# A decoder layer on one core: attention outputs divided two units at once, a later normalisation, outputs ahead of ranks at the end, and rows placed in three portions

## The reference

```python
# x, ctx: (128, 64, 128) f32; LN is layernorm without scale and shift
x = LN(x + self_attention(x))        # 8 heads, blocks of 64 rows, biases
x = LN(x + cross_attention(x, ctx))  # 16 heads of 8 columns, a mask of bytes
probs = softmax(x @ Wr.T)            # 8 experts
vals, idx = top_k(probs, 2); w = vals / vals.sum(-1)
h = silu(einsum('btd,efd->btef', x, W1)); y = einsum('btef,edf->bted', h, W2)
x = LN(x + sum over the two experts of w * y)
```

## Time and profile before

| | us |
|---|---|
| median of 3 runs (lowest to highest) | 1175.23 (1173.22 to 1178.68) |
| the profiled execution | 1175.13 |
| its span, first to last instruction | 1173.3 |

### The profile page before, as it was taken

The page is one execution under the profiler, slowest core; times in us unless marked ns, Lnnn a source line. Parts: engine busy times, 40 slices in busy tenths (PEclk is TensorE's granted clock), DMA queues, the critical chain, the costliest instruction groups (busy, mean ns, idle before and its releaser), DMA issues. The chain is left out here.

```text
span 1173.3 us, 31174 instructions
## 1 busy us (share of the span) xinstructions
PE 940.2 (80%) x11091; PEld 835.9 (71%) x11092; DVE 854.6 (73%) x2668; ACT 712.7 (61%) x1193; POOL 432.5 (37%) x527
## 2 busy tenths in 40 slices
PE   3888888888789989898989897685009999999991
PEld 2677776777678778787878686574009999999991
DVE  3687878788878888888888886666605767776772
ACT  3666667576477766666766556342007777877781
POOL 3142423324410111111111123543262777777674
PEclk9898889898899998999999979796559999999996
DMA  5940000000001000000000000000012322332220
GB/s 162 210 69 19 18 9 18 9 18 18 13 13 24 13 13 13 13 11 11 11 11 11 12 5 22 31 22 17 10 55 62 69 67 67 70 70 61 51 44 0
DMA packets 103727, 42.26 MB, mean 36 GB/s; under 512 B 58291, under 2 KB 99517, under 8 KB 103669
## 3 DMA queue, kind: packets, MB, share of 16 engines
q1 hardware_dynamic: 98676, 32.94, 13.8%
q0 software_dynamic: 4992, 8.54, 2.3%
HBM read 20.68 MB, written 16.57 MB: 32 GB/s over the span
## 5 line engine op out<-in xcount | busy, mean ns | idle before, releaser
L897 ACT ACTIVATE pr<-psum 128x512 f32<-128x512 f32 x192 | 114.1, 594 | 107.7 <-PE psum L604 102.7
L1107 DVE TENSOR_TENSOR at<-psum,rc 64x32 f32<-64x32 f32 (+1 forms) x768 | 153.5, 200 | 14.4
L1091 DVE TENSOR_REDUCE mx<-psum 128x8 bf16<-128x512 f32 x192 | 132.9, 692 | 36.3 <-PE psum L525 23.7
L901 ACT ACTIVATE pt<-psum 128x512 f32<-128x512 f32 x192 | 113.2, 589 | 66.9 <-PE psum L613 62.9
L501 POOL DMA_INDIRECT out_dram<-X,dest x92 | 122.8, 1335 | 65.1 <-ACT X L999 47.0
L613 PE MATMUL psum<-ident,pr 128*128 128x128 f32 x768 | 127.1, 291 | 14.8 <-ACT pr L897 11.5
L629 PE MATMUL psum<-vz_cross,pt 128*128 128x36 f32 x1024 | 133.2, 278 | 0.0
L629 PEld LDWEIGHTS psum<-vz_cross,pt 128*128 128x128 f32 x1024 | 131.3, 201 | 0.2
L604 PE MATMUL psum<-mx,negI 128*128 128x512 bf16 x192 | 77.4, 403 | 50.8 <-DVE mx L1091 46.8
L613 PEld LDWEIGHTS psum<-ident,pr 128*128 128x128 f32 x768 | 93.5, 151 | 29.5 <-ACT pr L897 20.7
L378 POOL TENSOR_SCALAR ve<-mv 128x4 f32<-128x4 f32 x55 | 19.5, 355 | 241.3 <-DVE mv L1241 224.6
(11 more groups left out here) (220 smaller groups left out, 3137.9 us busy)
## 6 DMA issues: line engine op xcount, KB each, us to landing
xd<-blank SPq DMA_DIRECT2D x1, 6072.0 KB, 37.5
X<-xd SPq DMA_DIRECT2D x23, 264.0 KB
X<-x_dram SPq DMA_DIRECT2D x16, 256.0 KB, 2.9
wst<-w_dram SPq DMA_DIRECT2D x16, 256.0 KB, 2.7
cin<-ctx_in_dram SPq DMA_DIRECT2D x16, 256.0 KB, 2.8
out_dram<-X,dest POOLq DMA_INDIRECT x92, 2.3
mraw<-mask_dram SPq DMA_DIRECT2D x32, 32.0 KB, 2.7
xd<-XTa,pos POOLq DMA_INDIRECT x64, 2.3
```

The source lines that it names most:

```text
L897: nc.scalar.activation(pr[u % 2][:], SC[u % 2][:], ACT.Exp).then_inc(s["ex"], 1)
L901: nc.scalar.activation(pt[u % 2][:], TB[u % 2][:], ACT.Copy).then_inc(s["ph"], 1)
L1091: nc.vector.tensor_reduce(mx[u % 2][:], SC[u % 2][:].rearrange("p (r k) -> p r k", k=S), AX.X, ALU.max).then_inc(s["mx"], 1)
L1107: m = nc.vector.tensor_tensor(dst, src, r, ALU.mult)
```

## The change

Four things are changed; the computed result is the same.

1. In cross-attention `norm` is called at even units only and divides the outputs of two units: one reciprocal of 32 columns and four products of 64 columns in place of two and eight. The two units share a PSUM bank, and the routing's results lie behind them (`lead`).
2. `finish` of cross-attention moves from unit 5 to 7 (`FIN`), RT from 4 to 3, RANK from 2 to 3 (read on DVE at 4, with `own_rank`), LG on PE from 6 to 5. On POOL `convert` of the mask goes behind `inv_std`.
3. The first table is sent in shorter first and longer second runs (6, 7, 7 and 4, 5, 6, 5 tiles), and it is finished later in group 12 (units 6 and 7 in place of 3 to 5).
4. The remaining 24 tiles become two portions, 16 (groups 10 to 13) and 8 (groups 14 and 15). In `closing` the last values, their `norm` and AT come first; the second portion's tables are made between them and the last `finish`, and its 16 sends are queued on POOL while DVE goes on to the third portion, which adds a table step of four linked instructions (`after_rows`).

```diff
-GA = 10
+CHUNKS = (0, 10, 14, 16)
-        lead = PVB[1][:, 144:]
+        lead = [PVB[1][:, 288:], PVB[0][:, 288:]]
@@ POOL
-                    if la.cross:
-                        convert(g, i)
...
                     if not first_group(g):
                         inv_std(g - 1, s["mv"], before, s["rs"])
-                    if late and g == GA + 2:
+                    if la.cross and follow >= 2:
+                        convert(g + 2, i)
+                    if late and g == first_tables:
...
+                    if la.cross:
+                        low_rows(G - 2)
                     inv_std(G - 1, s["mv"], before, s["rs"])
...
-            for h in range(G - 2, G):
-                low_rows(h)
+            pool.wait_ge(r_pos, 3)
+            send(range(chunk(1).start, chunk(1).start + 4))
+            low_rows(G - 1)
+            send(range(chunk(1).start + 4, chunk(1).stop))
             pool.wait_ge(r_lr, G)
             pool.wait_ge(r_pos, 4)
-            send(range(GA * GT, NT))
+            send(range(chunk(2).start, chunk(2).stop))
@@ PE
                 def closing():
+                    last_values()
                     RT(G - 2, G)
-                    last_values()
+                    AT(G - 1, 1)
+                    pe.wait_ge(r_s, PT * (NPAIR - 1))
+                    count(last_rk[0][:, PT * NP:])
                     rank(NPAIR - 2, last_rk[0])
                     logits(G - 2, last_lg[0])
-                    last_out()
+                    O(G - 1, 1)
                     RT(G - 1, G)
                     logits(G - 1, last_lg[1])
-                    rank(NPAIR - 1, last_rk[1], True)
+                    pe.wait_ge(r_s, PT * NPAIR)
+                    count(last_rk[1][:, PT * NP:])
+                    rank(NPAIR - 1, last_rk[1])
@@ DVE
                 def norm(g, u, i):
+                    many = 2 * HB if la.cross else HB
...
+                    nc.vector.reciprocal(recip, raw.rearrange("p (b jc e) -> p b jc e", b=many, jc=4)[:, :, :, la.dk]).then_inc(s["rc"], 1)
...
-                        if u > 0:
-                            norm(g, u - 1, i)
+                        if not la.cross or u % 2 == 0:
+                            if u > 0:
+                                norm(g, u - 1, i)
...
                 def closing():
+                    last["norm"]()
                     rl(G - 2)
-                    last["norm"]()
                     last["al"]()
+                    of_class(NPAIR - 2, last_rk[0])
+                    whole(1, last_rk[0][:, PT * NP:])
+                    own_rank(NPAIR - 2)
+                    gates_of(1)
                     last["stats"]()
-                    of_class(NPAIR - 2, last_rk[0])
-                    own_rank(NPAIR - 2)
                     keep(G - 2, 0, NPAIR - 1, last_lg[0])
+                    capacity(1)
+                    place_rows(1, 0)
                     last["finish"]()
                     rl(G - 1)
                     keep(G - 1, 1, NPAIR - 1, last_lg[1])
                     select(NPAIR - 1)
                     running_on(NPAIR - 1)
-                    gates_of(1)
+                    after_rows()
+                    gates_of(2)
                     of_class(NPAIR - 1, last_rk[1])
-                    whole(last_rk[1])
+                    whole(2, last_rk[1][:, PT * NP:])
                     own_rank(NPAIR - 1)
-                    capacity(1)
-                    place_rows(1, 0)
-                    place_rows(1, 1)
+                    capacity(2)
+                    place_rows(2, 0)
                     words()
...
-SENT_BEFORE = {12: range(0), 13: range(4, 12), 14: range(15, 24), 15: range(28, 37)}
-SENT_AFTER = {12: range(0, 4), 13: range(12, 15), 14: range(24, 28), 15: range(37, 40)}
-SLOTS = {"self": {"QK": 0, "V": 1, "AT": 1, "O": 2, "XT": 3},
-         "cross": {"QK": 0, "V": 2, "AT": 3, "O": 4, "XT": 5, "CT": 6, "HIGH": 1, "RANK": 2, "OWN": 3, "RT": 4, "LG": 6}}
+SENT_BEFORE = {12: range(0), 13: range(4, 10), 14: range(15, 22), 15: range(28, 35)}
+SENT_AFTER = {12: range(0, 4), 13: range(10, 15), 14: range(22, 28), 15: range(35, 40)}
+SLOTS = {"self": {"QK": 0, "V": 1, "AT": 1, "O": 2, "XT": 3, "FIN": 3},
+         "cross": {"QK": 0, "V": 2, "AT": 3, "O": 4, "XT": 5, "CT": 6, "FIN": 7, "HIGH": 1, "RT": 3, "RANK": 3, "LG": 5}}
```

More of the change, by code:

```diff
@@ L438, in opening @@
                         pool.wait_ge(sems["self"]["fin"], 2)
-                    ahead(0, 0)
-                    ahead(1, 1)
+                    for g in range(2):
+                        ahead(g, g)
+                        if la.cross:
+                            convert(g, g)
                 def body(g, i, follow, p):
                     route = la.cross and not (isinstance(g, int) and g < 2)
-                    late = la.cross and isinstance(g, int) and g >= GA + 2
+                    late = la.cross and isinstance(g, int) and g >= first_tables
                     if route:
@@ L619, in values @@
                     pe.wait_ge(s["ph"], n + 1)
-                    wait(pe, s["nm"], n - 1)
+                    if not la.cross:
+                        wait(pe, s["nm"], n - 1)
+                        dst = PVB[u % 2]
+                    else:
+                        if u % 2 == 0:
+                            wait(pe, s["nm"], g * (la.nh // 2) + u // 2 - 1)
+                        dst = PVB[u // 2 % 2][:, u % 2 * HB * W:]
                     if early:
@@ L669, in logits, with count, rank @@
                     m.then_inc(r_lg, 1)
-                def rank(p, dst, total=False):
+                def count(dst):
+                    nc.tensor.matmul(totals(dst), ones2[:, 0:P], S16[:, PT - 1, :], start=True, stop=True, skip_group_check=True).then_inc(r_count, 1)
+                def rank(p, dst):
                     pe.wait_ge(r_s, PT * (p + 1))
@@ L922, in body @@
                     for u in range(la.nh):
-                        if la.cross and u == 0 and isinstance(g, int) and g == GA + 2:
+                        if la.cross and u == 0 and isinstance(g, int) and g == first_tables:
                             odds_of(0)
@@ L1138, in body @@
                             stats(g - 1)
-                        if ranked and u == slot(la, "RANK"):
+                        if ranked and u == slot(la, "RANK") + 1:
                             dve.wait_ge(s["pv"], g * la.nh + u)
-                            of_class(p - 2, lead)
+                            of_class(p - 2, lead[0])
+                        if route and u == slot(la, "LG") + 1:
+                            dve.wait_ge(s["pv"], g * la.nh + u)
                             if tables:
-                                whole(lead)
-                        if route and u == slot(la, "LG"):
-                            dve.wait_ge(s["pv"], g * la.nh + u)
-                            keep(g - 2, i, p - 1, lead)
-                        if u > 0:
-                            norm(g, u - 1, i)
-                        elif not first:
-                            norm(g - 1, la.nh - 1, 1 - i)
+                                whole(0, lead[1][:, GT * E:])
+                            keep(g - 2, i, p - 1, lead[1])
+                        if not la.cross or u % 2 == 0:
+                            if u > 0:
+                                norm(g, u - 1, i)
+                            elif not first:
+                                norm(g - 1, la.nh - 1, 1 - i)
                         if u + 2 < la.nh:
@@ L1178, in body @@
                             classes(g + 1, 1 - i, la.class_slots[u])
-                        if u == slot(la, "O") + 1 and not first:
+                        if u == slot(la, "FIN") and not first:
                             finish(g - 1)
@@ L1251, in _ @@
             o = 24 + P
-            code, steps = cst[:, o:o + NP], cst[:, o + NP:o + 3 * NP]
-            lane_rows = cst[:, o + 3 * NP:o + 3 * NP + 1]
-            room, start, ends, more, shifted, ones_c, past, past_b = (tab[:, n] for n in (0, 1, 2, 4, 5, 6, 7, 8))
-            ends_both = tab[:, 2:4].rearrange("p n c -> p (n c)")
-            past_both = tab[:, 7:9].rearrange("p n c -> p (n c)")
+            code, steps = cst[:, o:o + NP], cst[:, o + NP:o + 4 * NP]
+            lane_rows = cst[:, o + 4 * NP:o + 4 * NP + 1]
+            room, start, more, shifted, ones_c = (tab[:, n] for n in (0, 1, 5, 6, 7))
+            ends = [tab[:, 2 + c] for c in range(3)]
+            past = tab[:, 8]
+            ends_all, past_all = (tab[:, n:n + 3].rearrange("p n c -> p (n c)") for n in (2, 8))
             def each(v):
@@ L1490 @@
     const[:, o:o + NP] = rows - 9 * E
-    const[:, o + NP:o + 2 * NP] = np.append(np.diff(rows), rows[0] - rows[-1])
-    const[:, o + 2 * NP:o + 3 * NP] = np.append(np.diff(rows), 0)
-    const[:, o + 3 * NP] = np.arange(P) * P
+    steps = [np.append(np.diff(rows), last) for last in [rows[0] - rows[-1]] * 2 + [0]]
+    const[:, o + NP:o + 4 * NP] = np.concatenate(steps)
```

(1 more changed line is left out.)

95 lines of the change are left out of this document (53 added, 42 removed).

## The result

| | before | after |
|---|---|---|
| median (lowest to highest), us | 1176.95 (1173.22 to 1181.73) | 1126.22 (1124.80 to 1128.54) |
| ratio to before, 95% interval | | 0.9569 (0.9527 to 0.9610) |
| the profiled execution | 1175.13 | 1127.16 |
| its span | 1173.3 | 1125.4 |

The changed kernel is 4.3% faster. First the page: busy time by engine, and three of its strips of 40 slices (28 us each).

What follows compares the result with a forecast made beforehand. Three costs beyond PE's own work: bursts on DVE, a stall in group 13, and 30 us of sends with all else idle. 12.0 + 2.4 + 9.8 + 16.5 = 40.7 us off 1175.13 gave 1134.4 us, range 1126 to 1142.

Steps and rivals of the forecast that it cites:

- rival (c): No delay of signals at the end and 5 us less of stalls in the runs of sends: 1127 us; chance 0.13.
- Six steps from even to odd: Cross-attention up to group 11: double `norm` and later `finish` save 2.0 us a step in PE stalls, 12.0 us together.
- The four steps after a `select`: Odd to even groups: 0.6 us gained four times, 2.4 us, though the stall of 2.44 becomes some 3.35.
- Groups 11 to 15: Late cross-attention: +0.8 for groups 11 to 13, +10.5 for 13 to 14, -1.5 for 14 to 15, together 9.8 us.
- the stall for `rstd`: Group 13: `finish` on DVE waits 8.40 us; this stall and the slow clock behind it go, 11 us.
- The price of the runs of sends: Late cross-attention: each run costs its length less 5 us, 14.3 us for the new runs against some 11 before.
- The end: Closing and its sends: bare gain 19.1 us, less 2.6 for delayed signals, gives 16.5 us.
- The 2.6 us for delayed signals: Third portion in `closing`: PE's signal for the ranks, inside a run of twelve sends, comes late and costs 2.6 us.
- Rival (b): Merging gives little in the loop because bursts shift: gain 3 us in place of 14.4, total 1146 us; chance 0.13.
- Rival (d): Third portion: DVE's linked steps each wait a send's pitch, 1.27 us in place of 0.26; total 1179 us; chance 0.02.

Runs made afterwards that it cites:

- run 2: The `norm` for two units alone, put into the kernel before, with only the first table's making moved besides: 1162.26 us, ratio 0.9881 to the kernel before.
- run 3: The changed kernel with `finish` of cross-attention back at unit 5, all else as changed: 1147.29 us, ratio 0.9747 to the kernel before.
- Run 4: The kernel before with one move, POOL's cast of the mask put behind `rstd`: 1173.59 us, ratio 0.9972 to the kernel before.
- run 8: The changed kernel with the mask's cast back ahead of the sends and `rstd` on POOL, second chip: 1101.75 us, ratio 0.9595 to the kernel before.
- run 7: The changed kernel with the sends of groups 13 to 15 meant to be spread over units, second chip: 1094.07 us, ratio 0.9559 to the kernel before.
- run 9: Both kernels once more, unaltered, on the third chip: changed kernel 1098.85 us, kernel before 1147.77 us, ratio 0.9598.

## Why the prediction was right, and where it was not

The total, 1126.2 us for 1134.4, lies in the range, at its lower end, and beside rival (c). Of the two reasons of (c) one holds (no delay of signals at the end); the other (5 us less of stalls in the runs) doesn't, as the stalls were longer. By the profiles the gain is 47.9 us for 40.7, and part of the surplus is luck: 3.9 us came up to group 0, which the third chip doesn't repeat, and 2.8 in the steps behind a `select`, where the third chip has 0.2 us for the 5.2.

- *Six steps from even to odd, 2.0 us each*: right. 24.69 to 24.85 us, no stall left, 11.7 us in sum. The reciprocal of 32 columns took 0.35 us where I took 0.28, the products 0.93; there was room. On the third chip it is 11.7 again. What I had not seen is that the gain hangs on the late `finish`: run 2 has only 0.55 us of the 2.0, and run 3, with `finish` in its old place, 0.4.
- *The four steps after a `select`*: the stall grew to 3.21 us as predicted (3.35), and a new one at unit 7 is 0.27 where I had 0.65. The term came to 5.2 us for 2.4. Where both kernels have the same clock a step gives 1.0 us, where 0.6 had been predicted. But one step of the kernel before (9 to 10, 32.68 us, clock 0.84) had 2.2 us of slow clock in it, and one of the changed kernel (3 to 4, 31.68 us, clock 0.84) as much, with 0.89 there before. On the third chip the four steps give 0.3, 0.8, -0.6 and -0.3, 0.2 us in sum, as the slow clock falls mostly on two steps of the changed kernel. For the clock behind a stall the term had no allowance at all, and it can be as large as the term.
- *Groups 11 to 15*: the stall for `rstd` went, as predicted. Run 4 shows that the cast's place removes it by itself; run 8 that with the cast ahead the shorter run and the later `finish` leave 3.42 us of the 8.40. The price of the runs of sends, their length less 5 us, was mis-sized: I had 14.3 us for the five new runs, and the third chip, without such waits, shows what the first paid: 23 us, of it 4.2, 7.0 and 12.5 in the steps to groups 13, 14 and 15 (less 0.7 in the one before), where I had 2.6, 5.2 and 6.5. It hid because the kernel before paid 17 of the same kind, 16 of them in the last two steps, where I had 11. It was read as a property of the kernel, which it is not. Where it is missing, the gain of the whole stretch is 13.5 us (126.27 less 112.80), and on the first chip 7.4.
- *The end*: the layout on the old clock held within 1 us. Places 20.2 us after unit 7 of group 15 (predicted 20.4) and 39.3 (38.4), last send 51.7 (52.0). The 2.6 us for delayed signals was wrong: no wait named remote stands in the closing, in either profile of the changed kernel. That is why the end gave 18.9 us for 16.5. That `finish` beside sends takes 1.14 us, not 1.95, is seen here again.
- *3.9 us up to group 0* were not predicted and aren't the change's: on the third chip the same stretch is 3.2 us longer after (345.05 and 348.27 for unit 7 of group 0). So it lies within what two single profiles differ by.
- *Rival (b)*, that bursts shift and eat the gain, is what happens to run 3; in the full change the order avoids it. Rival (d) did not show: DVE's linked steps beside sends keep their pitch of 0.26 us, but for the one beside `low_rows`.

## What to carry to other kernels

Moving a block of work on an engine that runs in bursts can be worth as much as making it shorter (12.5 us on top of the rest here, 11 for the shorter `norm` alone), and moving other blocks without it can cost (run 3): look for the gap between two tops that the block sits in, and move it to the pair with room. Where an order of outputs is free, finish a first portion's tables before the last result is needed, so that the slow issue of sends runs under the rest. A wait whose releaser the trace does not name should be looked for on a second chip before it is priced as part of a kernel. After an edit that is meant to move work in time, read in the trace whether the work has moved (run 7).

## What the runs showed of the hardware

- *The same program on several chips.* The kernel before took 1177, 1145 and 1148 us, the changed one 1126 and 1099. Beside the waits in runs of sends (17 and 23 us), the part behind the last send took 299 us on the first chip and 289 on the third, in both kernels.
- *One stall, three prices.* In run 9 (the changed kernel) PE waits 3.20 us for the same top in groups 6, 8 and 10, and the steps take 29.51, 31.14 and 32.35 us. By stretches, in that order:

```profile
474.88:504.39 29.51, 26.05 (x274) 23.02 (x273) 23.72 (x75) 19.08 (x36) 5.31 (x14) 0.94 0.06 11
```

```profile
529.25:560.39 31.14, 27.68 (x274) 24.50 (x273) 23.95 (x75) 19.14 (x36) 5.31 (x14) 0.89 0.05 11
...
585.25:617.60 32.35, 28.88 (x275) 25.30 (x274) 23.61 (x75) 19.25 (x36) 5.32 (x14) 0.84 0.05 10
```

The work is equal, the mean granted clock is 0.94, 0.89 and 0.84. The same stall costs up to 2.8 us more of slow clock in one group than in another, and nothing in the rows ahead of it tells which. It isn't the chip: on the second one the four steps behind a `select` take 28.9, 29.5, 31.2 and 32.3 us in run 8, as here, and 31.7, 29.4, 29.5 and 29.5 in run 7, as on the first. A term of a sum should have room for that.

- *DVE beside POOL.* One step of `select` took 1.50 us (799.51, in the closing above) where 0.23 is usual, beside `low_rows(15)` on POOL (799.76 to 800.92). The sends around it delay no step. By the Trainium skill (SBUF — State Buffer, "Who interferes with whom") the two engines share their ports as an exclusive lock; the trace agrees for POOL's tensor operation, and shows no such lock beside its sends.
